# A two-layer decoder on one core: the norm of the second attention, and the product keys of its memory layer

## The reference, cut to what matters

```python
residual = h
mu = jnp.mean(h, axis=-1, keepdims=True)
var = jnp.mean(jnp.square(h - mu), axis=-1, keepdims=True)
x = (h - mu) * jax.lax.rsqrt(var + EPS) * ln_g + ln_b
q = (x @ wq.T + bq).reshape(b, s, N_HEADS, D_K)      # k and v likewise
...
return o @ wo.T + bo + residual
```

```python
queries = (hidden_states @ W_q).reshape(2, n, RETRIEVAL // 2)
```

## Time and profile before

| | us |
|---|---|
| median of 3 runs | 1073.08 |
| lowest, highest | 1072.37, 1073.54 |
| the profiled execution | 1073.45 |
| its span | 1071.7 |
| PE busy | 1007.0 |
| DVE busy | 743.6 |
| ACT busy | 622.7 |
| POOL busy | 402.7 |

### The profile page before, as it was taken

One profiled execution on the slowest core, in us unless ns is written; L12 is line 12 of the kernel. 1 busy time (PEld: TensorE's weight loads), 2 busy tenths in 40 slices (PEclk: granted clock), 3 DMA queues, 4 the chain that ended last, 5 costly groups with the idle time before them and its releaser, 6 DMA issues. The chain is left out here.

```text
span 1071.7 us, 21337 instructions
## 1 busy us (share of the span) xinstructions
PE 1007.0 (94%) x7186; PEld 833.7 (78%) x7186; DVE 743.6 (69%) x2168; ACT 622.7 (58%) x1559; POOL 402.7 (38%) x380
## 2 busy tenths in 40 slices
PE   8999999999998988899998999999999988889988
PEld 7677887877776557788887788888898875777867
DVE  6677777777755687555557677776777763748984
ACT  2188777777773863333443677777777764224332
POOL 5766667676643011000002635343434421111240
PEclk9999999999999999999998999999999999989999
DMA  5361122201006000654430101110110100001101
GB/s 174 70 189 36 36 60 51 55 17 41 2 2 225 2 2 20 122 139 110 103 83 6 31 16 31 34 29 25 28 36 15 30 6 1 1 1 45 45 30 55
DMA packets 25916, 53.65 MB, mean 50 GB/s; under 512 B 3986, under 2 KB 11218, under 8 KB 24558
## 3 DMA queue, kind: packets, MB, share of 16 engines
q1 hardware_dynamic: 25838, 52.65, 18.7%
HBM read 42.56 MB, written 1.69 MB: 41 GB/s over the span
## 5 line engine op out<-in xcount | busy, mean ns | idle before, releaser
L522 ACT ACTIVATE sb_a_P<-sb_a_nS,sb_a_nm 128x257 f32<-128x257 f32 x256 | 127.6, 507 | 86.5 <-DVE sb_a_nm L633 86.3
L432 POOL TENSOR_TENSOR sb_a_P<-sb_a_P,sb_a_rec 128x512 f32<-128x512 f32 x128 | 129.2, 1040 | 87.6 <-DVE sb_a_rec L644 87.4
L633 DVE CUSTOM_DVE_ANT_0 sb_a_nS<-a_pS,sb_a_mask,sb_a_nsink 128x256 f32<-128x256 f32 x256 | 109.3, 479 | 39.7 <-PE a_pS L781 39.7
L1940 ACT ACTIVATE sb_a_t<-a_pp,sb_a_w 64x512 f32<-64x512 f32 x128 | 87.4, 683 | 17.0 <-PE a_pp L143 9.4
L2013 DVE SCALAR_TENSOR_TENSOR sb_a_t<-a_pp,sb_a_w,sb_a_cs 128x512 f32<-128x512 f32 x64 | 47.8, 746 | 56.0 <-ACT sb_a_t L1940 56.0
L143 PE MATMUL a_pp<-sb_x_high,sb_a_w_low 128*128 128x512 f32 x188 | 80.6, 429 | 5.7 <-DVE sb_a_P L588 3.5
L1879 POOL TENSOR_TENSOR sb_a_qT<-sb_a_t 128x512 f32<-128x512 f32 x32 | 41.3, 1292 | 116.1 <-DVE sb_a_t L2016 116.1
L143 PE MATMUL a_pp<-sb_x_low,sb_a_w_high 128*128 128x512 f32 x188 | 75.0, 399 | 0.0
L143 PE MATMUL a_pp<-sb_x_high,sb_a_w_high 128*128 128x512 f32 x188 | 74.9, 398 | 0.0
L531 ACT COPY sb_xn<-a_pT 128x512 f32<-128x512 f32 x128 | 68.0, 583 | 1.9 <-PE a_pT L795 1.9
L795 PE MATMUL a_pT<-sb_ident,sb_a_P 128*128 128x128 f32 x512 | 68.2, 276 | 0.3 <-ACT sb_xn L531 0.3
(11 more groups left out here) (416 smaller groups left out, 3178.7 us busy)
## 6 DMA issues: line engine op xcount, KB each, us to landing
sb_m_cw<-m_table SPq DMA_DIRECT2D x15, 512.0 KB
sb_a_kr<-sb_a_kall SPq DMA_DIRECT2D x28, 256.0 KB, 3.9
sb_f_w<-f_w SPq DMA_DIRECT2D x12, 384.0 KB, 3.1
sb_m_gu<-m_gu SPq DMA_DIRECT2D x17, 256.0 KB, 6.3
sb_a_w<-a_w SPq DMA_DIRECT2D x16, 257.0 KB, 2.7
sb_m_dn<-m_dn SPq DMA_DIRECT2D x17, 128.0 KB, 7.0
sb_a_w<-a_w SPq DMA_DIRECT2D x8, 259.0 KB, 2.7
sb_a_wo<-a_wo SPq DMA_DIRECT2D x8, 256.0 KB, 2.6
```

Of the source, the lines that this page charges most:

```text
L432: nc.gpsimd.tensor_tensor(part, part, rec[b % 2][:, h, :].rearrange("p (q o) -> p q o", o=1) .to_broadcast([P, 2, S]), ALU.mult).then_inc( ...
L522: out = nc.scalar.activation(Pm[b % 2][:, h, qt, 0:S + 1], nS[:, h, qt, 0:S + 1], ACT.Exp, bias=nm[b % 2][:, h, qt:qt + 1], scale=-1.0, ac ...
L633: out = nc.vector.tensor_tensor_reduce(nS[:, h, qt, 0:S], pS[h][:, qt * S:(qt + 1) * S], wmask[:, qt, :], -1.0, nsink[par][:, h:h + 1], AL ...
L1940: out = nc.scalar.activation(t2[n][a, :, :].rearrange("p b s -> p (b s)"), pp[n][b, :], ACT.Identity, bias=bias[b])
```

## The change

In attention_1:

- ln_g and ln_b come as columns (`a1_cols`, one value for each partition of the transposed form) and no longer as rows; `a1_rows` is replaced by `a1_bo` and `a1_cols`.
- DVE's two instructions for each tile become one: subtract the mean, multiply by the inner root. ln_g and ln_b are applied where the turned rows are copied out of PSUM into k.xT: three of the four pieces on ACT, one on DVE. The casts and the low parts read k.xT.
- POOL makes the inner root of a half first, and then the outer one, in two `pow`s of half the size.
- `grow` moves on ACT, two tiles at a time, behind each of the first head's four swaps; `grown` and `shift` move on DVE behind the low parts.

In memory_1:

- `QI` has 128 partitions: half 0 on the lower 64, half 1 on the upper 64; the keys lie likewise. The key products of the two sets take turns, one on the lower and one on the upper half of the array's rows.
- They start after the gate product of half 0; its up product moves behind them. They wait for all four copies of `QI` at once.
- POOL's first `w_low` waits until all normed rows are ready.

```diff
-        exponents = k.minus_half[:, :].rearrange("p (a n) -> p a n", a=2)
+        exponents = k.minus_half[:, 0:HALF]
+        outer, both = self.spread2[:, 0, cols], self.spread2[:, 1, cols]
         pool.wait_ge(self.ln, (half + 1) * 2 * HALF)
...
+        nc.gpsimd.tensor_scalar(both, k.mv[:, cols, 1], 1.0 + LN_EPS, LN_EPS * LN_EPS, ALU.mult, ALU.add)\
             .then_inc(self.rstd_ready, 1)
+        pool.wait_ge(self.rstd_ready, 4 * half + 1)
+        nc.gpsimd.tensor_tensor(self.root2[:, 1, cols], both, exponents, ALU.pow).then_inc(self.rstd_ready, 1)
+        nc.gpsimd.tensor_scalar(outer, k.mv[:, cols, 1], LN_EPS, None, ALU.add).then_inc(self.rstd_ready, 1)
+        pool.wait_ge(self.rstd_ready, 4 * half + 3)
+        nc.gpsimd.tensor_tensor(self.root2[:, 0, cols], outer, exponents, ALU.pow).then_inc(self.rstd_ready, 1)
...
-            for half in range(2):
-                grow(half)
-                act.wait_ge(turned, half + 1)
-                for j in (half, 2 + half):
-                    high_of(nc, part_of(k.xs[0], j), turn_banks[j][:, :]).then_inc(x_high, 1)
+            def turned_row(j):
+
+                d = j // NH2
+                act.wait_ge(turned, j % NH2 + 1)
+                nc.scalar.activation(part_of(k.xT, j), turn_banks[j][:, :], ACT.Identity, bias=cols_of[:, 1, d:d + 1],
+                                     scale=cols_of[:, 0, d:d + 1]).then_inc(affine, 1)
+
+            def high_row(j):
+                high_of(nc, part_of(k.xs[0], j), part_of(k.xT, j)).then_inc(x_high, 1)
+
+            turned_row(0)
+            turned_row(2)
+            act.wait_ge(affine, 2)
+            high_row(0)
+            high_row(2)
+            turned_row(3)
+            act.wait_ge(affine_by_vector, 1)
+            high_row(1)
+            act.wait_ge(affine, 3)
+            high_row(3)
...
             for c in range(4):
                 swap(0, 0, c)
+                grow(c)
...
+            for half in range(2):
+                dve.wait_ge(rstd_ready, 4 * half + 2)
                 for t in range(half * HALF, (half + 1) * HALF):
...
+                    nc.vector.tensor_scalar(k.xn[:, t, :], k.x[:, t, :], k.mv[:, t, 0:1], root2[:, 1, t:t + 1],
+                                            ALU.subtract, ALU.mult).then_inc(xn_ready, 1)
+            dve.wait_ge(turned, 2)
+            nc.vector.tensor_scalar(part_of(k.xT, 1), turn_banks[1][:, :], cols_of[:, 0, 0:1], cols_of[:, 1, 0:1],
+                                    ALU.mult, ALU.add).then_inc(affine_by_vector, 1)
+            for i, j in enumerate((0, 2, 1, 3)):
+                dve.wait_ge(x_high, i + 1)
+                low_of(nc, part_of(k.xs[1], j), part_of(k.xT, j), part_of(k.xs[0], j)).then_inc(xT_ready, 1)
             for half in range(2):
-                centre(half)
                 cols = slice(half * HALF, (half + 1) * HALF)
-                dve.wait_ge(rstd_ready, 2 * half + 2)
-                dve.wait_ge(centred, (half + 1) * HALF)
+                dve.wait_ge(rstd_ready, 4 * half + 4)
...
-        QI = sb("QI", [F1_R, T, 2])
+        QI = sb("QI", [2 * F1_R, NC, 2])
...
+            pool.wait_ge(k.norm_of_f1.xn_ready, NT)
             for n in range(TILES):
                 pool.wait_ge(w_high, n + 1)
...
-            gate_up(0, (0,))
-            for a in range(2):
-                pe.wait_ge(QI_ready, 2 * a + 2)
-                for j in range(NT):
-                    rows_n = QI[:, a * NC + j * (P // 2):a * NC + (j + 1) * (P // 2), :].rearrange("r t s -> r (t s)")
-                    out = nc.tensor.matmul(acc[a][:, j * F1_KEYS:(j + 1) * F1_KEYS], rows_n, keys[:, a, :],
+            gate_up(0, (0,), (0,))
+            pe.wait_ge(QI_ready, 4)
+            for j in range(NT):
+                for a in range(2):
+                    strip = slice(a * F1_R, (a + 1) * F1_R)
+                    rows_n = QI[strip, j * (P // 2):(j + 1) * (P // 2), :].rearrange("r t s -> r (t s)")
+                    out = nc.tensor.matmul(acc[a][:, j * F1_KEYS:(j + 1) * F1_KEYS], rows_n, keys[strip, :],
                                            start=True, stop=True)
             out.then_inc(routed, 1)
+            gate_up(0, (0,), (1,))
             gate_up(0, (1,))
```

More of the change, by code:

```diff
@@ L63 @@
            ("x1_decay", [P, 2, 3 * P], F32), ("x1_rows", [P, 2, D], F32)],
-    "f1": [("f1_wq", [P, KD, P], F32), ("f1_keys", [64, 2, 64], F32), ("f1_iota", [P, 512], F32)]
+    "f1": [("f1_wq", [P, KD, P], F32), ("f1_keys", [P, 64], F32), ("f1_iota", [P, 512], F32)]
           + [(f"f1_w{i}", [P, 3 * D], F32) for i in range(3)],
@@ L1728, in attention_1 @@
         cmask = k.tile["a1_mask"]
-        rows = k.tile["a1_rows"]
+        bo, cols_of = k.tile["a1_bo"], k.tile["a1_cols"]
         qT = [sb(f"qT{i}", [P, T]) for i in range(2)]
@@ L1898, in _ @@
                 pool.wait_ge(grown_x, t + 1)
-                nc.gpsimd.tensor_tensor(k.x[:, t, :], k.x[:, t, :], rows[:, 2, :], ALU.add).then_inc(based, 1)
+                nc.gpsimd.tensor_tensor(k.x[:, t, :], k.x[:, t, :], bo[:, :], ALU.add).then_inc(based, 1)
             heads(pool, step)
@@ L1916, in _, with grow @@
             k.wait(act, "a1")
-            def grow(half):
-                act.wait_ge(shifts, half + 1)
-                for t in range(half * HALF, (half + 1) * HALF):
+            def grow(c):
+                act.wait_ge(shifts, c // 2 + 1)
+                for t in (2 * c, 2 * c + 1):
                     nc.scalar.activation(k.x[:, t, :], k.x[:, t, :], ACT.Identity, bias=shift[:, t:t + 1],
                                          scale=grown[:, t:t + 1]).then_inc(grown_x, 1)
-            for half in range(2):
-                grow(half)
-                act.wait_ge(turned, half + 1)
-                for j in (half, 2 + half):
-                    high_of(nc, part_of(k.xs[0], j), turn_banks[j][:, :]).then_inc(x_high, 1)
+            def turned_row(j):
[15 more added lines that the diff above has]
+            high_row(3)
             def swap(X, par, c):
@@ L1999, in _ @@
                                                op0=ALU.mult, op1=ALU.mult).then_inc(shifts, 1)
[L2000 to L2005, removed]
             def rope(X, par, c):
@@ L2563, in _ @@
                 for s in range(2):
-                    nc.scalar.copy(QI[:, half * NC:(half + 1) * NC, s], acc[2 + half][s * F1_R:(s + 1) * F1_R, :])\
+                    nc.scalar.copy(QI[half * F1_R:(half + 1) * F1_R, :, s], acc[2 + half][s * F1_R:(s + 1) * F1_R, :])\
                         .then_inc(QI_ready, 1)
@@ L2763, in _, with gate_up @@
                 out.then_inc(queried, 1)
-            def gate_up(n, halves=range(2)):
+            def gate_up(n, halves=range(2), parts=range(2)):
                 pe.wait_ge(w_split, n + 1)
@@ L2769, in gate_up @@
                         pe.wait_ge(h_ready, 2 * n + h - 1)
-                    for bank, off in ((pg[h], 0), (pu[h], D)):
+                    for part in parts:
+                        bank, off = (pg, pu)[part][h], part * D
                         if off and n >= F1_GT:
@@ L2783, in gate_up @@
                                                       PW[:, 4 * h + t, e * P:(e + 1) * P], k.tile["ident"][:, :])
-                    out.then_inc(gated, 1)
+                    if 1 in parts:
+                        out.then_inc(gated, 1)
             def down(n):
@@ L2913, in layouts @@
     out["a1_mask"] = np.concatenate([above, np.zeros((P, P), f), above], axis=1)
-    out["a1_rows"] = np.stack([both(a["L1_attn_" + n]) for n in ("ln_g", "ln_b", "bo")], axis=1)
+    out["a1_bo"] = both(a["L1_attn_bo"])
+    out["a1_cols"] = np.stack([a["L1_attn_" + n].reshape(KD, P).T for n in ("ln_g", "ln_b")], axis=1)
     hw = lambda wt: wt.reshape(A1_H, P, KD, P).transpose(0, 3, 2, 1).reshape(A1_H, P, KD * P)
@@ L2935, in layouts @@
     out["f1_wq"] = rowm(a["L1_ffn_W_q"])
-    out["f1_keys"] = a["L1_ffn_keys"].transpose(1, 0, 2)
+    out["f1_keys"] = a["L1_ffn_keys"].reshape(P, -1)
     out["f1_iota"] = np.broadcast_to(np.arange(F1_E, dtype=f), (P, F1_E))
```

14 lines of the change are left out of this document (3 added, 11 removed).

## The result

The changed kernel takes 1069.92 us (median of 12 runs, 1064.58 to 1074.93); the kernel before took 1074.12 in the same session (12 runs, 1072.37 to 1081.39). The ratio is 0.9948, 95% interval [0.9925, 0.9971]: faster by 0.5%. The profiled execution of the changed kernel took 1072.43 us, its span 1070.6, at a mean granted clock of 0.983 (before: 1073.45, 1071.7, 0.984).

What follows compares the result with a forecast made beforehand. PE works 94% of the span; memory_1 hangs on the keys' end (961.22), then DVE's routing. attention_1's 0.9 and memory_1's 3.75 sum to 4.65 us, taking the median 1073.08 to 1068.4; range 1065.8 to 1071.2.

Steps and rivals of the forecast that it cites:

- Part 1, rows to projection: attention_1's norm: the first projection starts at 583.15 instead of 584.99, -1.85 us; bounds -2.1 and -1.2.
- Part 1, growing copies: attention_1: grow pairs queued behind the swaps on ACT make three steps 7.2 us instead of 6.28, +0.9; bounds 0, +1.1.
- rival C: Clock high where it was low, in memory_1's queries or the first projections: 1.5 to 2 us faster, 1066.7; chance 0.13.
- Part 2: memory_1's rows: w_low waiting for all normed rows ends its collision with DVE's rows, -0.9 us; bounds 0 and -1.2.
- Part 3: memory_1's order: keys start at 955.4 instead of 956.6, ahead of half 0's up product, -1.2 us; bounds -0.9, -1.4.
- Part 4: memory_1's 32 key records in two alternating row strips take 2.05 us instead of 3.71, -1.65; bounds 0 and -1.85.
- A: memory_1's key strips don't overlap, 116 ns a record stay; gives 1.65 us back, 1070.1; chance 0.12.
- E: memory_1's alternating strips don't pipeline, each key record takes its 274 ns latency: slower, 1075.2; chance 0.05.
- Behind the keys: memory_1 after the keys: DVE stays the bound, hT(1)'s silu has 0.3 us to spare, 11.8 us to the last spread.
- Rival B: Clock falls behind memory_1's keys, slowing records hT(1) waits for: 1.6 us less 0.3 added, 1069.7; chance 0.16.
- Rival D: POOL's pows shut out DVE's rows in attention_1, projection starts 1.1 us later: 1069.5; chance 0.10.
- the rest shifts as it is: memory_1 behind the keys: DVE goes on as the bound and the remaining work only moves earlier, at unchanged length.

Runs made afterwards that it cites:

- order and wait alone: Kernel before with only memory_1's new order of products and w_low's wait for the normed rows, keys in the old layout: 1072.33 us, ratio 0.9985.
- the changed kernel with 224 bytes: Changed kernel plus 224 bytes of padding per partition, putting experts_0's weight parts at 128 past a multiple of 256 bytes: 1066.86 us, ratio 0.9919.
- the attention_1 part alone with 224 bytes: Kernel before with only the change's attention_1 edits, plus 224 bytes of padding per partition: 1072.55 us, ratio 0.998.
- the strips alone: Kernel before with only the new QI and keys' layout and alternating key records; order, w_low and attention_1 as before: 1071.66 us, ratio 0.9972.
- the fillers: Changed kernel with 96 bytes of padding, plus extra unread transposes in PE's idle gaps in attention_1 and memory_1: 1068.52 us, ratio 0.9936.
- the spread `grow` with 96 bytes: Changed kernel with 96 bytes of padding, one grow behind each of the first three swaps, five behind the fourth: 1072.05 us, ratio 0.9934.

## Why the prediction was right, and where not

The time (1068.4 forecast, 1069.92 measured in a session whose kernel before stood 1.04 over the one I started from) is right, and so are the mechanisms of parts 2 to 4. That the total came so near, 4.2 us of gain for 4.65, is in part luck: in the traces the edited stretches won 6.3 us (1.9 in attention_1, 4.4 in memory_1), more than the sum had, and code whose time I had taken as fixed moved by 6.26 us the one way and 0.91 the other. Step by step:

- **Part 1, rows to projection, -1.85.** Measured -1.88, by the steps named: rows done after 2.9 us, affine copies 0.77 to 0.81 (0.75 taken), the pitch 0.68 (0.67 taken).
- **Part 1, growing copies, +0.9.** With the clock low in the first row block, the new kernels need 14.29 to 14.67 us from projection to scores, 0.9 to 1.2 over the 13.43 of before, which had it low too (the other kernels with the old attention_1: 13.34 to 13.94). With the clock high they need 13.45, and the profile of the changed kernel had it high: 0.0. ACT is the bound there, as forecast (steps of 2.52; I had 2.40, with 1.02 for a pair of `grow`s that takes 1.09). So rival C came true in this place, and its gain was the 0.9 that the growing copies cost.
- **Part 2, -0.9.** Measured -0.94, in the kernel with order and wait alone, too. No row of 1349 ns is left.
- **Part 3, -1.2.** Measured -1.53, outside its own bounds (-0.9 and -1.4). The keys stood 6.57 us behind the queries' start where I had put 7.0: ACT's last two `QI` copies run from 957.16 to 958.40, the keys start at 958.46, and pg ends at the same time. I had rounded these hand-overs up by 0.3, and the queries took 5.24 instead of 5.39, since the clock rose before their last record. The term is not firmer than the clock: the same stretch took 7.12 in the memory_1 part alone and 7.11 in the changed kernel with 224 bytes (clock 0.57 and 0.58, here 0.63), and 4.29 to 4.35 in the four kernels whose queries had the clock at 1.00. That is rival C's other place, and it never came in the five kernels with the old order (7.40 to 8.10).
- **Part 4, -1.65.** Measured -1.77: 2.04 us from first key record to the copy of R. Two strips give the 64 ns a record that four gave. Rivals A and E are out.
- **Behind the keys.** The forecast had hT(1) with 0.3 to spare and DVE as the bound; the stretch took 10.97 us, 0.15 less than before. Both hold, the spare time barely: ACT's silu of half 1 ends at 965.49, and hT(1) begins less than 0.1 us later. In the kernel before, hT(1) had waited for it (the two took 1.41 us, here 1.26), which is the 0.15. Rival B did not come in the changed kernel, but it is a real mechanism: in the attention_1 part alone with 224 bytes the clock fell during the keys, and keys and the stretch behind took 4.38 and 11.97 us, 0.57 and 0.85 over those of before.
- **Rival D.** Eight rows in 2.84 us beside a `pow` of 1.21, none over 422 ns: no blocking. The Trainium skill (SBUF — State Buffer, "Who interferes with whom") has it for DVE instructions in a two-port mode; the trace shows it for `w_low` next to the norm's rows alone. That the rows were in such a mode is not shown: line 207's four take 1.38 us, a pitch of 0.33, and DVE's subtraction of two tensors of the same 256 columns, the one for wq, has 0.34. So the collision and its end are shown, its reason is not.
- **The range.** Its lower end does not follow as the text has it: C (1066.7) with part 1 at -2.1 instead of -0.9 is 1065.5, not 1065.8. The measured time is far from it.

What failed is the sentence that the rest shifts as it is, and with it the tacit step that code ahead of the change keeps its time. The change makes two resident tiles smaller (by 2016 and 256 bytes a partition), and everything placed behind both moves by 2272 bytes. That costs experts_0, which nobody touched, 1.7 us in 14 tiles (a little more may lie in the tiles outside the 14, which the clock hides). This is shown: the same 1.7 appears with 32 bytes of padding in the kernel before and goes with 224 bytes in the changed one. attention_1's heads gain 0.64 by the same shift (0.44 in the kernel before), so that the traces' net cost is 1.0 to 1.2 us, some 0.1% of the time. The runs agree with that but don't prove it (ratios 0.9948 without and 0.9919 with 224 bytes; their intervals overlap).

The rest of the 6.26 us lost ahead of attention_1 in the profiled execution is the clock, as far as the rows tell: the mean over 414 to 468 us is 0.87, in the kernel before 0.97, and a clock lower by 0.10 over 54 us can cost up to 5.4 us (an estimate from these two figures). Placement is not needed for it: the memory_1 part alone and the strips alone have the tile at 8.34, and their attention_1 starts at 580.80 and 581.77, 4.2 and 5.1 us behind the kernel before, the order alone at 577.23. Whether it differs by execution or by kernel, one profile of each can't tell.

For each part alone the measured gain is more than the direct one. In the mean over all runs the two parts alone (attention_1 with 224 bytes, memory_1) are 3.5 and 6.1 us under the kernel before, where the changed kernel's stretches give 1.9 and 4.4 us; against the kernel before of their own sessions it is 2.5 and 6.6. Along with that the runs' mean clock goes from 0.9811 to 0.9849 and 0.9862. At equal clock, though, they are 0.1 over and 1.4 under the kernel before, less than the stretches show, so that the fit puts too much down to the clock and does not settle the shares. That less idle time of PE brings the higher clock is argued, not shown: the fillers held it high in the one place where the base's profile had it low, and won no time in the median.

What stays open: why the 512-column records prefer one place of the four seen in 256 bytes (other places than 0, 128, 160 and 192 were not tried, nor was the moving of one tile alone, so that it need not be the weights' place that counts), what a part of the change is worth in whole runs, and what decides whether the clock falls behind the keys, since either of two edits removes it.

## What to carry to other kernels

Price each step against the next thing that is late: with every engine's queue around the moved instructions counted, four of the five steps held to 0.33 us, and the fifth where the clock was as assumed. When a change alters the size of a resident buffer, compare the pace of untouched loops before and after first; an unnoticed shift of addresses cost one loop here as much as the strips won. And when two builds differ in which stretches run at the low clock, compare stretches at the same clock, and take whole runs of both in the same session.

## What the runs showed of the hardware

- Where the buffers of experts_0 start within a partition matters: with its weight parts at 128 past a multiple of 256 bytes a record of 512 columns takes 389 to 392 ns, at 0, 160 and 192 it takes 394 to 396 (14 kernels); no difference for 256 columns (282 to 283).
- Two row strips of 64 in turns give 61 to 64 ns for a record of 64 columns, 116 to 119 in one strip at full clock.
- An affine copy of 128x512 out of PSUM with scale and bias by pointer takes 0.77 us on ACT and 0.81 on DVE.
- POOL's subtraction of 128x512 held up one of DVE's rows of 256 columns (1349 ns against 408), POOL's `pow`s of 128x4 none of eight (at most 422).
- The runs of this kernel follow their mean granted clock with -0.94 us per +0.001 (a fit over 231 runs); the runs of one build (the spread `grow` with 96 bytes) lay between 0.979 and 0.993.
- The same code, with experts_0's buffers at the same place within 256 bytes, ended up to 5.1 us apart in two profiled executions (attention_1 at 576.63 and 581.77; mean clock over 414 to 468 us 0.97 and 0.84).
